# Keeping the ternary second weight in SBUF instead of in DRAM scratch

## The reference

```python
xn = layernorm(x)
out = x + attention(xn) + ffn(xn)

def ffn(x):                       # FF = 4096
    h = gelu(x @ ternary(W1).T + b1)
    return h @ ternary(W2).T + b2

def ternary(w):                   # w: W1 (FF, 1024) or W2 (1024, FF)
    scale = max(mean(abs(w)), 1e-8)
    return clip(round(w / scale), -1, 1)
```

## Time and profile before

| | |
|---|---|
| Median of 3 runs | 1486.28 us (1481.68 to 1489.62) |
| The profiled execution's own time | 1487.05 us |
| Its span, slowest core | 1485.3 us (core 4) |
| Spans of the 8 cores | 1467.4 to 1485.3 us |
| PE busy | 990.5 us, 67% of the span |
| DVE busy | 548.0 us, 37% |
| ACT busy | 526.3 us, 35% |
| POOL busy | 93.7 us, 6% |
| DMA traffic | 167.06 MB, mean 112 GB/s |

### The profile page before, as it was taken

The page is one execution under the profiler, slowest core; times in us unless marked ns, Lnnn a source line. Parts: engine busy times, 40 slices in busy tenths (PEclk is TensorE's granted clock), DMA queues, the critical chain, the costliest instruction groups (busy, mean ns, idle before and its releaser), DMA issues.

```text
span 1485.3 us, 21169 instructions; the slowest of 8 cores (1467.4 to 1485.3 us)
## 1 busy us (share of the span) xinstructions
PE 990.5 (67%) x6696; PEld 504.7 (34%) x6696; DVE 548.0 (37%) x1279; ACT 526.3 (35%) x886; POOL 93.7 (6%) x155
## 2 busy tenths in 40 slices
PE   0000229988788788888725935888788506999995
PEld 0000004455455455456412312333333203344442
DVE  2122210057788677777744454222222100001000
ACT  0344443365656765866741202333332200000000
POOL 1111100000000000000000001111111100010010
PEclk9999659999998989998967977999999857999998
DMA  9789960000000011011038844555444554655762
GB/s 186 237 258 235 239 174 4 1 2 5 5 2 6 2 19 19 2 19 34 1 53 217 283 170 149 168 151 166 147 152 151 172 178 109 157 142 118 181 149 35
DMA packets 120295, 167.06 MB, mean 112 GB/s; under 512 B 40064, under 2 KB 91264, under 8 KB 116096
## 3 DMA queue, kind: packets, MB, share of 16 engines
q0 software_dynamic: 24928, 97.53, 24.0%
q1 hardware_dynamic: 95264, 68.19, 17.0%
HBM read 119.56 MB, written 41.94 MB: 109 GB/s over the span
## 4 chain that ended last, share of the span: by engine, by line
PE 34%; DMA 32%; DVE 16%; issue 10%; ACT 4%; POOL 1%; SPq 1%; DVEq 1%; PEld 0%; ACTq 0%; POOLq 0%; PEldq 0%
DMA wst<-w2T 11%; PE psS L835 8%; DMA p1st<-w1T 6%; PE psS L761 6%; PE psS L692 5%; DMA hg_ts<-hg_scr 4%; DMA p1st<-w2T 4%; PE psY L723 4%; DVE pv L441 4%; DMA w_sb<-w2t_scr 3%; PE psY L835 3%; PE psY L742 3%; ACT A_buf L626 2%; PE psS L799 2%; PE psY L799 2%
## 5 line engine op out<-in xcount | busy, mean ns | idle before, releaser
L626 ACT ACTIVATE A_buf<-psS,consts 128x512 bf16<-128x512 f32 (+3 forms) x427 | 276.3, 712 | 158.7 <-PE psS L761 155.9
L813 PE MATMUL psS<-xnT,w_sb 128*128 128x512 bf16 x1024 | 230.6, 383 | 79.1 <-ACT hgst L659 40.1
L761 PE MATMUL psS<-qh_ext,kT 128*128 128x512 bf16 (+3 forms) x640 | 172.5, 349 | 66.9 <-DVE A_buf L445 34.9
L441 DVE TENSOR_SCALAR pv<-psS 128x512 bf16<-128x512 f32 (+3 forms) x213 | 129.5, 608 | 159.6 <-PE psS L761 157.3
L813 PEld LDWEIGHTS psS<-xnT,w_sb 128*128 128x128 bf16 x1024 | 98.4, 98 | 210.7 <-issue 100.4
L835 PE MATMUL psS<-w_sb,hg_ts 128*128 128x512 bf16 x512 | 115.9, 389 | 67.5 <-DMA hg_ts<-hg_scr 67.5
L692 PE MATMUL psS<-xnT,wq_bf 128*128 128x512 bf16 x64 | 21.5, 509 | 203.3 <-DMA xnT<-xn_tm 203.3
L659 ACT ACTIVATE hgst<-psS,consts 128x512 bf16<-128x512 f32 x128 | 84.9, 685 | 182.0 <-DMA hg_scr<-hgst 114.4
L723 PE MATMUL psY<-v_tm,A_buf 128*128 128x64 bf16 x2176 | 119.2, 192 | 18.8 <-DVE A_buf L456 5.7
L723 PEld LDWEIGHTS psY<-v_tm,A_buf 128*128 128x128 bf16 x2176 | 98.6, 97 | 45.2 <-issue 30.7
L761 PEld LDWEIGHTS psS<-qh_ext,kT 128*128 128x128 bf16 x640 | 60.0, 96 | 157.1 <-issue 140.9
(11 more groups left out here) (100 smaller groups left out, 759.2 us busy)
## 6 DMA issues: line engine op xcount, KB each, us to landing
p1st<-w1T POOLq DMA_DIRECT2D x16, 1024.0 KB, 7.4
p1st<-w2T POOLq DMA_DIRECT2D x16, 1024.0 KB, 8.5
wst<-w1T POOLq DMA_DIRECT2D x16, 1024.0 KB, 8.2
wst<-w2T POOLq DMA_DIRECT2D x32, 512.0 KB, 4.8
hg_scr<-hgst SPq DMA_DIRECT2D x128, 128.0 KB, 2.7
hg_ts<-hg_scr SPq DMA_DIRECT2D x32, 512.0 KB, 8.2
x_roll<-x SPq DMA_DIRECT2D x16, 512.0 KB, 10.4
out<-out_sb SPq DMA_DIRECT2D x16, 512.0 KB, 5.8
```

Source lines behind the costliest of these rows:

```text
L441: pub(e.tensor_scalar(pv[:, slot, 0:w], psS[idx % 4][:, 0:w], SC, BI, ALU.mult, ALU.add))
L626: e.activation(A_buf[:, gs % 4, t0:t0 + w], psS[idx % 4][:, 0:w], AF.Square, bias=cc(C_CBI), scale=cc(C_CSC)).then_inc(sPOLY, 1)
L761: e.matmul(psS[idx % 4][:, 0:w], kT[:, h // 8, m * 128:(m + 1) * 128], qh_ext[:, hi, t0:t0 + w], start=True, stop=True).then_inc(sSC, 1)
L813: mm = e.matmul(ps[:], w12_sb[:, c * FF + j * 128:c * FF + j * 128 + 128], xnT[:, 4 * tb:4 * tb + 4, c, :], start=(c == 0), stop=(c == KD ...
```

## The change

The ternary second weight gets a place of its own in SBUF, `w2t_sb` (64 KB per partition, at 96 to 160 KB). VectorE's subtraction writes there, and the second product reads it there. The stores to `w2t_scr` and the 32 reads back go away, with their semaphores; TensorE's first 32 matmuls of the second product wait for VectorE's count `sW2T` instead. To make the room, `hg_ts` moves to 32 KB, over the first weight; `wst` to 176; the comparison results `jw2a`, `jw2b` to 160 and 164; `b2_bf` and `hgst` both to 201. VectorE waits once more for the end of the output projection before the first tile of the second weight, since `w2t_sb` lies over `wo_bf`.

```diff
--- before.py
+++ after.py
@@ -50,7 +50,6 @@
     w2T_d = nc.dram_tensor("w2T", [FF, D], F32, kind="ExternalInput").ap()
     b2_d = nc.dram_tensor("b2r", [1, D], F32, kind="ExternalInput").ap()
     out_d = nc.dram_tensor("out", [T, D], F32, kind="ExternalOutput").ap()
-    w2t_scr = nc.dram_tensor("w2t_scr", [32, 128, D], BF16, kind="Internal").ap()
     hg_scr = nc.dram_tensor("hg_scr", [32, 128, T], BF16, kind="Internal").ap()
 
     SBUF_BASE = 16512
@@ -63,8 +62,9 @@
     w12_sb = at("w12_sb", [128, 32768], BF16, 32)
     jw1a = at("jw1a", [128, 2, T], BF16, 144)
     jw1b = at("jw1b", [128, 2, T], BF16, 152)
-    jw2a = at("jw2a", [128, 2, D], BF16, 96)
-    jw2b = at("jw2b", [128, 2, D], BF16, 100)
+    jw2a = at("jw2a", [128, 2, D], BF16, 160)
+    jw2b = at("jw2b", [128, 2, D], BF16, 164)
+    w2t_sb = at("w2t_sb", [128, 32, D], BF16, 96)
     p1st = at("p1st", [128, 2, T], F32, 32)
     x_roll = at("x_roll", [128, 6, D], F32, 64)
     ajunk = at("ajunk", [128, T], BF16, 88)
@@ -75,13 +75,12 @@
     xn_tm = at("xn_tm", [128, NT, D], BF16, 96)
     y_tm = at("y_tm", [128, 4, NT, 128], BF16, 96)
     wo_bf = at("wo_bf", [128, KD, D], BF16, 96)
-    b2_bf = at("b2_bf", [1, D], BF16, 112)
-    hgst = at("hgst", [128, 2, 512], BF16, 114)
+    b2_bf = at("b2_bf", [1, D], BF16, 201)
+    hgst = at("hgst", [128, 2, 512], BF16, 201)
     v_tm = at("v_tm", [128, NT, D], BF16, 128)
-    wst = at("wst", [128, 2, T], F32, 128)
-    hg_ts = at("hg_ts", [128, 2, 32, 256], BF16, 128)
+    wst = at("wst", [128, 2, T], F32, 176)
+    hg_ts = at("hg_ts", [128, 2, 32, 256], BF16, 32)
     pv = at("pv", [128, 2, 512], BF16, 188)
-    w2tb = at("w2tb", [128, 2, D], BF16, 152)
     wq_bf = at("wq_bf", [128, KD, 256], BF16, 168)
     qT = at("qT", [128, 2, T], BF16, 160)
     junk = at("junk", [128, 2, D], BF16, 160)
@@ -156,7 +155,7 @@
     sYTT = S("sYTT"); dYTT = DS("dYTT"); sWOG = S("sWOG"); sWOGs = S("sWOGs")
     sWO = S("sWO"); sWOE = S("sWOE"); dOUT1 = DS("dOUT1"); dXRE = DS("dXRE")
     dW1L = DS("dW1L"); sW1T = S("sW1T")
-    dW2L = DS("dW2L"); sW2T = S("sW2T"); dW2S = DS("dW2S"); dW2F = DS("dW2F")
+    dW2L = DS("dW2L"); sW2T = S("sW2T")
     sH = S("sH"); sHGs = S("sHGs"); dHGW = DS("dHGW"); dHGR = DS("dHGR")
     sO2 = S("sO2"); sO2E = S("sO2E"); dOUT2 = DS("dOUT2")
 
@@ -249,12 +248,6 @@
             dHGW.inc(e.dma_start(out=hg_scr[j][:, tb * 512:(tb + 1) * 512],
                                  in_=hgst[:, i % 2, :]), i)
         e.wait_ge(sH, 128)
-        dW2S.wait_all(e, 32)
-        for j in range(32):
-            if j >= 2:
-                dW2F.wait_done(e, j - 2)
-            dW2F.inc(e.dma_start(out=w12_sb[:, j * D:(j + 1) * D],
-                                 in_=w2t_scr[j]), j)
         for k in range(8):
             dHGW.wait_all(e, 32 * (k // 2 + 1))
             if k >= 1:
@@ -308,8 +301,6 @@
                 e.wait_ge(sW2T, j - 1)
             dW2L.inc(e.dma_start(out=wst[:, j % 2, 0:D],
                                  in_=w2T_d[j * 128:(j + 1) * 128, :]), j)
-            e.wait_ge(sW2T, j + 1)
-            dW2S.inc(e.dma_start(out=w2t_scr[j], in_=w2tb[:, j % 2, :]), j)
         dOUT1.wait_all(e, NT)
         for t in (0, 1):
             dXRE.inc(e.dma_start(out=x_re[:, t, :],
@@ -531,16 +522,16 @@
 
         for j in range(32):
             e.wait_ge(sTHR, 10)
+            if j == 0:
+                e.wait_ge(sWO, 2 * NT)
             dW2L.wait_done(e, j)
-            if j >= 2:
-                dW2S.wait_done(e, j - 2)
             src = wst[:, j % 2, 0:D]
             pub(e.tensor_single_scalar(jw2a[:, j % 2, :], src, cc(C_T2),
                                        ALU.is_gt))
             pub(e.tensor_single_scalar(jw2b[:, j % 2, :], src, cc(C_T2N),
                                        ALU.is_lt))
             fence()
-            e.tensor_tensor(w2tb[:, j % 2, :], jw2a[:, j % 2, :],
+            e.tensor_tensor(w2t_sb[:, j, :], jw2a[:, j % 2, :],
                             jw2b[:, j % 2, :],
                             ALU.subtract).then_inc(sW2T, 1)
         dOUT1.wait_all(e, NT)
@@ -831,11 +822,11 @@
                     e.wait_ge(sO2E, i - 3)
                 for j in range(32):
                     if ts == 0 and dh == 0:
-                        dW2F.wait_done(e, j)
+                        e.wait_ge(sW2T, j + 1)
                     mm = e.matmul(ps,
                                   hg_ts[:, k % 2, j,
                                         (ts % 2) * 128:(ts % 2) * 128 + 128],
-                                  w12_sb[:, j * D + dh * 512:j * D + (dh + 1) * 512],
+                                  w2t_sb[:, j, dh * 512:(dh + 1) * 512],
                                   start=(j == 0), stop=(j == 31))
                 mm.then_inc(sO2, 1)
```

## The result

The changed kernel takes 1420.95 us (median of 10 runs, 1408.33 to 1434.89), against 1485.88 us for the kernel before in the same runs. Some executions are slowed by a lower clock on one die, or otherwise stand over 1.5% above the fastest; the medians contain them, while every ratio here leaves them out. The ratio is 0.9532, with a 95% interval of 0.9493 to 0.9572: 4.7% faster. The forecast was 1424.5 us and 4.2%. By the ratio the changed kernel stands at 1416.3 us (0.9532 x 1485.88), so the forecast was 8.2 us too slow, and not only the 3.6 us by which the median differs.

A forecast was written before the change was run, and what follows sets the result against it. No single bound: no line held over 11% of the chain. 1487.05 - 48.35 (gap) - 13.4 (first product's stalls) = 1425.3 us profiled, less 0.77 for the median: 1424.5 us, 4.2% faster; range 1403 to 1442 us.

The forecast's parts named there:

- The gap, 48.35 us: Between the products: without the 32 reads, the first hidden read goes out at about 1176.9 instead of 1225.25, gaining 48.35 us.
- The ternary weight is never waited for: Second product's start: waiting for VectorE's subtraction costs nothing, as the ternary loop ends near 1020 us.
- The first product, 13.4 us: First product: TensorE's waits for gelu fall from 40.1 to 26.7 us, a gain of 13.4 us.
- 1.67 us per MB: First product: TensorE's loss per MB moved by the ternary loop, 40.1 us over 24 MB, applied to the 16 MB left.
- In between: First product: the value by bytes, taken between nothing gained and nearly all of the 40.1 us coming back.
- R2: First product: stalls nearly vanish, 512 KB alone not pushing stores past 2.7 us; some 5 us stay, 1403 us; chance 0.15.
- R3: Ternary loop: VectorE holds up the loads, which come singly as 512 KB bursts; 11 us of stalls, 1409 us; chance 0.07.
- R1: First product: gelu's stores suffer as before, the same 40 us of stalls in its first 110 us; 1438 us; chance 0.21.
- R4: First product: stores under two loads land so late that they pace it; slower, 1518 us; chance 0.02.
- R5: Between the products: something else holds the first hidden read, only the stalls' gain is left; 1473 us; chance 0.03.
- The second product, unchanged: Second product: same 1024 matmuls and reads, first matmuls slow as before; it takes 248.6 us again.
- Some stalls outlive the loads: First product: TensorE's waits for gelu lie before 1030 us, none after; stalls continuing after the loads would show the forecast wrong.

The follow-up runs named there:

- the serial version: Changed kernel with one load of the second weight in flight: 1442.62 us with stores of the ternary tiles put back, 1411.71 us without them.

## Why the prediction was right

**The gap, 48.35 us.** Right in size and place. Measured 59.8 - 11.4 = 48.4 us (medians of 8 cores). This is shown from both sides: with only the reads gone the gap is 14.7, with only the reads kept 61.5 us. The hidden read stayed exposed, forecast 11.45 and measured 11.4 us.

**The ternary weight is never waited for.** Right. Tile `wst` shows the loads' first and last start:

```profile
...
L302 POOL DMA_DIRECT2D wst<-w2T x32: 530/530/1000, 906.3 to 1022.0; - x32
...
```

They run at (1022.0 - 906.3)/31 = 3.7 us each, the last ternary tile ends near 1029 (forecast near 1020), 134 us before the second product.

**The first product, 13.4 us.** The direction was right, the size too small: 20.2 us, with 20.0 us of waits left where 26.7 were forecast. The step that failed is the price: "1.67 us per MB", stalls in proportion to bytes. Three results speak against it. With the same 16 MB, one load in flight costs 13.7 and 11.2 us and two cost 20.0. With the same 24 MB, one in flight costs 38.2 and two cost 30.5. And with the same 16 MB, one more staging buffer leaves 3.2. The forecast of the whole came within 8.2 us all the same because the gap, which was priced from its own rows, makes up 48.35 of the 61.75 us of the sum. In place of the price by bytes the runs show that a store costs nothing up to a certain lateness, and what lies beyond in full. TensorE waits, medians of 8 cores:

| | one load in flight | two loads in flight |
|---|---|---|
| loads alone (16 MB) | 13.7, again 11.2 | 20.0, again 20.0 |
| with a store or an extra load (24 MB) | 38.2, extra load 36.1 | 30.5 |

A store of gelu is delayed by what is queued beside it at that time. Two buffers hide a landing of up to 2.7 us, and TensorE has some 0.75 us of slack behind a late gelu; both figures are the prediction's, 3.45 us together. The traces hold the issue and the landing of every gelu store, so what its 128 stores land later than 3.45 us can be added up on each core (medians of 8 cores):

| | landings beyond 3.45 us, sum | TensorE waits |
|---|---|---|
| kernel before | 43.0 | 39.5 |
| stores put back, one load in flight | 41.7 | 38.2 |
| extra load | 38.9 | 36.1 |
| stores put back, two loads in flight | 37.0 | 30.5 |
| changed kernel, twice | 22.1, 21.7 | 20.0, 20.0 |
| one load in flight, twice | 13.0, 11.0 | 13.7, 11.2 |

The two columns agree within some 10%, but for the run with stores and two loads, where the sum is 6.5 us too high. With a third buffer a store may land one tile (1.73 us) later, 5.18 us: beyond that stand 2.5 us, and 3.2 were measured. So lateness less slack, store by store, is the price that holds. A burst of 512 KB goes little beyond the slack (90% of the stores during the ternary loop land within 3.8 us with one load in flight); with the 256 KB more that went out before, whichever way they moved, it is 4.6 us, and all of the addition counts. That is why removing a third of the bytes took 24.5 us of stalls in the serial version (38.2 to 13.7), and not a third of 38.

**"In between", and R2.** The value was chosen between two bounds, and the measured one lies between it and R2. The argument made for R2, that a smaller burst may fit into the slack of nearly 1 us, is the right mechanism. R2 as stated, 5 us left, wasn't reached: even single loads leave 11 to 14 us, and the second load in flight adds 6 to 9. The argument against R2 had it that two loads go out 2.2 us apart. That step was wrong too: they spread. In the timeline of the changed kernel loads go out at 1002.07, 1005.65 and 1009.19:

```profile
...
1002.07 0.53 POOL L302 DMA_DIRECT2D wst<-w2T  x1 [3.15 <-DVE w2t_sb L534]
...
1003.48 0.69 ACT L650 ACTIVATE hgst<-psS,consts 128x512 bf16<-128x512 f32 x1 [1.90 <-DMA hg_scr<-hgst]
...
1005.65 0.53 POOL L302 DMA_DIRECT2D wst<-w2T  x1 [3.05 <-DVE w2t_sb L534]
...
1007.00 0.69 ACT L650 ACTIVATE hgst<-psS,consts 128x512 bf16<-128x512 f32 x1 [1.56 <-DMA hg_scr<-hgst]
...
1009.19 0.53 POOL L302 DMA_DIRECT2D wst<-w2T  x1 [3.02 <-DVE w2t_sb L534]
...
```

They are 3.5 to 3.6 us apart, as far as two tiles of TensorE's, so that each pair of stores meets one (gelu waits for a store at 1003.48 and again at 1007.00). But a load takes 4.6 us to land in the median, so one is still under way when the next goes out. The landings show what that does: with two loads in flight a core has 14 stores that land later than 4 us, with one load only 6, while the stores later than 2.7 us are not more (37 against 42 of 128). That the second load in flight costs 6 to 9 us is shown by the runs; that it does so by making stores later, not more of them late, is what the landings show.

**R3** priced the case of single loads, at 11 us of stalls and 1409 us, by taking two thirds of one store's delay and then the slack. The run with one load in flight measured 13.7 and 11.2 us, and 1411.7 and 1411.4 us. So R3's working of lateness less slack was the one to use for the forecast as well. That VectorE holds up the loads, as R3 supposed, didn't come about: the page gives 4.6 us to landing in the median, against 4.8:

```profile
...
wst<-w2T POOLq DMA_DIRECT2D x32, 512.0 KB, 4.6
...
```

**R1** (the stalls stay at 40 us) and **R4** (slower) fell with the measurement; **R5** (the gap stays) too.

**The second product, unchanged.** Nearly: 2.8 us shorter by the medians. The slow first matmuls are the same, as forecast: its first two banks take 15.7 us in both (medians of 8 cores, from the first weight load into `psS` to the first into `psY`), and 15.8 with the 61.5 us gap kept, so it doesn't matter whether the idle is 11 or 60 us. TensorE's later waits for hidden chunks sum to 3.1 in place of 3.9 us, and from the last matmul to the end of the span it takes 13.7 in place of 15.6 us (medians of 8 cores). Why the end is shorter isn't traced; the whole 2.8 us is 0.2% of the time.

**Some stalls outlive the loads.** The prediction named this as a sign of being wrong, and "none after" 1030 was wrong by a little: on the slowest core TensorE waits 3.4 of 18.1 us after the loop's end:

```profile
...
PE psS L804 <- ACT hgst L650: 3.4, 3, 2.5
```

With nearly no loads 2.6 us stay as well. They come at single stores some 25 us apart. The traces show what moves beside those: a transfer of 16 KB on the queue that the page calls `instruction`, eight times per core during the first product. With nearly no loads, from 25 us behind the second load on, 66 of the 68 stores of all cores that land later than 2.6 us run beside such a transfer. The stores beside one land in 2.9 us in the median, the others in 1.8. That these transfers cause it is read from this coincidence; no run leaves them out. The loads themselves have ended by then. Three buffers or eight cover most of it. The page's row (packets, MB, share):

```profile
...
q8 instruction: 60, 0.98, 0.3%
...
```

**The other two signs** stayed away: while two loads fly, stores land in 3.0 us in the median (over 5 would have been wrong), and the first hidden chunk takes 11.4 us (over 16).

## What to carry to other kernels

Where a double-buffered store is in step with a matmul pipeline, price its disturbance as lateness less slack, store by store, and not by bytes: the last 256 KB of a burst may cost most of it, and one more buffer (here 1 KB per partition) won 22.1 us of the first product, this change 20.2. A DRAM round trip between two stages costs its reads in full when nothing else can run there; look next at the first read of what remains, and whether a place for it comes free before the stage ends. Fewer transfers in flight can be the faster choice where nobody waits for the loop that issues them.

## What the runs showed of the hardware that was not expected

A 256 KB load into SBUF disturbs gelu's stores to DRAM as much as a 256 KB store to DRAM does (36.1 against 38.2 us of waits). The Trainium skill, "DMA: Bandwidth & Descriptors" (Queues, rings and completion order), has each DMA engine take turns between the queues; that rule makes no difference between directions, and these two numbers agree with it. But the bound that the prediction drew from it, a loss between 26.7 and 40 us with two loads queued, did not hold: 20.0 us were measured.

After idle stretches of 11 and of 60 us, TensorE's first two banks of 32 matmuls took the same 15.7 and 15.8 us, where two undisturbed ones take 13.81. On every core of the kernel before and of the changed one the granted clock is at its lower level (0.5) over the first 2 to 6 us of them. Inside the first product of the changed kernel, a wait of TensorE's of 2.1 to 3.4 us stood beside each of the eight stretches of 3.4 us at the lower level.

A small transfer that the kernel doesn't issue, 16 KB on the instruction queue, stands beside a store that lands in 2.9 us in place of 1.8.
